# Relative attention on one core: content products moved to the free 64 rows, value products issued before the position products

## The chip, the cores and the metric

The program runs on one NeuronCore of one Trainium2 chip. The metric is the device time of one execution in microseconds (us); lower is better. The engines are PE (TensorE: matrix products, with its weight loads listed apart as PEld), DVE (VectorE), ACT (ScalarE), POOL (GpSimd) and SP (SyncE, which only issues transfers). SBUF is the on-chip working memory, PSUM the eight banks that PE writes its products into. A PE weight array has 128 rows, over which a product sums, and 128 columns, one per output row; a product may use only a part of either.

## The reference

The reference is a small network over x of shape (8, 512, 128): an attention block, a causal attention with a mixture of experts, a relative attention, and a low-rank feed-forward block, each with a layer norm. The change touches only the relative attention. Cut to what matters, for each of 8 sequences and 16 heads of width 8:

```python
AC = jnp.einsum('bhid,bhjd->bhij', q + u_bias[None, :, None, :], k)      # content
BD = jnp.einsum('bhid,hjd->bhij', q + v_bias[None, :, None, :], rp)      # positions
BD = _rel_shift(BD)
attn = jax.nn.softmax((AC + BD) * scale, axis=-1)
out = jnp.einsum('bhij,bhjd->bhid', attn, v)
```

## The kernel before

The program is a row of phases, each with its own semaphores and buffers; a phase starts when the one before has ended on all engines. `phase_relative` (from L1737) is the phase of the change. It works in 32 steps (8 sequences by 4 groups of 4 heads). A step has 16 tiles u = 0 to 15: tile u is head u // 4 and block u % 4 of 128 queries, against all 512 keys. The first four steps and the last four are written out, the 24 between them are a loop of six passes of four steps (`steps`, L1799).

Queries and keys are split into bf16 terms stacked to 48 rows (SK), so a product over 48 rows gives the float32 product. Four kinds of PE work occur in each step n:

- content (`content_tile`, L1920): one product of 128 queries with 512 keys into PSUM bank ps_ac[u % 2]. The tiles qu and k have 128 rows: rows 0 to 47 hold the stacks, and the rest are zeros set once by DVE at the start of the phase (L2056 to L2058). The product sums over all 128 rows.
- turn (`turn_tile`, L1927): four 128x128 float32 transposes of the finished scores into ps_keys[u % 2].
- positions (`wide_bank`, L1911): bf16 products of 48 rows by 32 columns, 8 to 20 of them to a bank of 512, for step n + 2. The queries with the v bias (qv) lie in rows 0 to 47 for even steps and in rows 64 to 111 for odd ones; the positions r are stored in both places. ACT copies each bank out (`copy_wide`, L1988), sends it to DRAM in two halves a step (`send`, L1993), and SP fetches it back skewed by one element a row (`fetch`, L1831), which is the relative shift. It lands in `shifted`.
- value (`value_head`, L1938): 32 float32 products of 128 rows by 9 columns per head, at u = 5, 9, 13 and, for the last head, at u = 1 of the next step.

For each tile DVE adds content and shifted positions with the row maximum (L2043) and subtracts the maximum (L2051); ACT takes the exponential of the turned tile (L2009). PE waits with content tile u + 2 for DVE to be done with tile u (two ps_ac banks), with turn tile u for L2051 of u and for the exponential of u - 2, and with a value head for the exponentials of its head, the last of them that of tile u - 2. A positions bank waits for ACT to have copied the bank three before it.

The order on PE is written out by hand. For each u of a step, cut to its calls:

```python
content_tile(n, s, u + 2)          # or the first two tiles of step n + 1
turn_tile(n, s, u)
wide_bank(n + 2, (j + 2) % NG, s, u // HT, u % HT)   # twice at u = 7 and 15
if u == 1 and not first:
    value_head(n - 1, 1 - s, G - 1)
if u % NT == 1 and u > NT:
    value_head(n, s, u // NT - 1)
```

SP issues, in order: at the start qv for two steps, ident, r (L1866), then a wait for all three settings of DVE (pad_set) and the stacks of step 0 (`load`, L1817 and L1819); in each step the stacks of the next step once the last head of the step before is done, the results, and the two fetches, each behind waits for the sending and for the turns that free its buffer.

Of the kernel before, what the change touches and what calls it, by code (L numbers as in the profile page):

```python
# [5 lines left out]
F32 = mybir.dt.float32  # L6
# [7 lines left out]
P = 128  # L14
NB = 8
L = 512
NT = L // P
H = 16
DH = 8
G = 4  # L20
# [5 lines left out]
SK = DH * len(TERMS_Q)  # L26
# [110 lines left out]
def phase_attention(nc, sems, x_in, w_qkvT, w_fcT, b_fc, gamma, beta, ident_in, x1_out, z1_out):  # L137

    SCALE = P ** -0.5
    with ExitStack() as ctx:
# [472 lines left out]
def phase_causal(nc, sems, q_stacks, k_stacks, v9_in, mask_in, maskT_in, ident_in, ctx_out):  # L615

    SCALE = DH ** -0.5
    ROWS = 64  # L620
# [1116 lines left out]
def phase_relative(nc, sems, qu_stacks, qv_stacks, k_stacks, v9_in, r_stack, ident_in, skew_dram, ctx_out):  # L1737
# [2 lines left out]

    SCALE = DH ** -0.5
    BANK = 512
    NBK = -(-CW // BANK)
# [2 lines left out]
    ROWS = 64  # L1748
    LOWEST = -3.0e38
    assert NBK == HT + 1 and NBK % BANKS == 0 and STEP == NG  # L1750
    with ExitStack() as ctx:  # L1751
        def sb(name, shape, dt=F32):
            return ctx.enter_context(nc.sbuf_tensor("r_" + name, shape, dt))
# [8 lines left out]
        qu = sb("qu", [P, 2, G, L], BF16)  # L1762
        k = sb("k", [P, 2, G, L], BF16)
# [10 lines left out]
        ps_ac = [bank("ps_ac0"), bank("ps_ac1")]  # L1774
# [4 lines left out]
        pad_set = sem("pad_set")  # L1779
# [33 lines left out]
        @block.sync  # L1813
        def _(sp):
            def load(it, j):
                for dst, src in ((qu, qu_stacks), (k, k_stacks)):
                    sp.dma_start(dst[0:SK, j % 2, :, :],  # L1817
                                 src.rearrange("b r (g h) t -> b g r h t", h=G)[it, j]).then_inc(loaded[j % 2], 16)
                sp.dma_start(v9[:, j % 2, :, :], v9_in.rearrange("b p t (g v) -> b g p t v", g=NG)[it, j])\  # L1819
                    .then_inc(loaded[j % 2], 16)  # L1820

            def load_queries(it, j):
                at = ROWS * (j % 2)
                sp.dma_start(qv[at:at + SK, :, 0:L], qv_stacks.rearrange("b r (g h) t -> b g r h t", h=G)[it, j])\
                    .then_inc(qv_loaded[j % 2], 16)

            def fetch(it, j, c):

                sp.wait_ge(sent[j % 2][c], 16 * uses(it, j))
                src = skew_dram[j % 2][c]  # L1830
                sp.dma_start(shifted[:, j % 2, HT * c:HT * (c + 1), :],  # L1831
                             bass.AP(tensor=src.tensor, offset=src.offset + P - 1, ap=[[CW - 1, P], [W, HT], [1, L]]))\
                    .then_inc(skewed[j % 2][c], 16)

            def after(it, j, by):
                return it + (j + by) // STEP, (j + by) % STEP

            def step(it, j, first, left):
                n = STEP * it + j
                if left >= 1:  # L1840
                    sp.wait_ge(head_done, G * n + 2)
                    load(*after(it, j, 1))
                if not first:
                    store(n - 1)
                if left >= 1:
                    if not first:
                        sp.wait_ge(keys_ps, TG * n)
                    fetch(*after(it, j, 1), 1)
                if left >= 2:
                    sp.wait_ge(keys_ps, TG * n + HT)  # L1850
                    fetch(*after(it, j, 2), 0)
                if left >= 4:
                    sp.wait_ge(wide_ps, 2 * NBK * (n + 3))
                    load_queries(*after(it, j, 4))

            def store(n):
                sp.wait_ge(out_sb, n + 2)
                for b in range(NT):
                    sp.dma_start(ctx_out[n, :, :, b * P:(b + 1) * P].rearrange("h r i -> r h i"),
                                 osb[Q * b:Q * b + VW, :, :]).then_inc(stored, 16)  # L1860

            load_queries(0, 0)
            load_queries(0, 1)
            sp.dma_start(ident[:, :], ident_in).then_inc(consts, 16)
            for s in range(2):
                sp.dma_start(r[ROWS * s:ROWS * s + SK, :, :, :],  # L1866
                             r_stack.rearrange("r (o g h) t -> g r o h t", g=2, h=G)[s]).then_inc(r_loaded, 16)
            sp.wait_ge(pad_set, 3)
            load(0, 0)
            sp.sem_inc(stored, 64)  # L1870
            for c in range(2):
                fetch(0, 0, c)
            sp.wait_ge(wide_ps, 2 * NBK)
            load_queries(0, 2)
            fetch(0, 1, 0)
            sp.wait_ge(wide_ps, 4 * NBK)
            load_queries(0, 3)
            steps(step, sp)
            store(NI - 1)
            for s in range(2):  # L1880
                sp.wait_ge(loaded[s], 48 * (NI // 2))
                sp.wait_ge(qv_loaded[s], 16 * (NI // 2))
                for c in range(2):
                    sp.wait_ge(sent[s][c], 16 * (NI // 2))
                    sp.wait_ge(skewed[s][c], 16 * (NI // 2))
            sp.wait_ge(r_loaded, 32)
            sp.wait_ge(stored, 64 * (NI + 1))

        @block.tensor
        def _(pe):  # L1890
# [26 lines left out]
            def content_tile(n, s, u):  # L1917
                h, b = u // NT, u % NT
                pe.wait_ge(ac_used, TG * n + u + 1)
                pe.matmul(ps_ac[u % 2][:, :], qu[:, s, h, b * P:(b + 1) * P], k[:, s, h, :], start=True, stop=True)\  # L1920
                    .then_inc(ac_ps, 1)

            def turn_tile(n, s, u):
                pe.wait_ge(s_ready, TG * n + u + 1)
                pe.wait_ge(exp_done, TG * n + u + 1)
                for j in range(NT):
                    last = pe.transpose(ps_keys[u % 2][:, j * P:(j + 1) * P],  # L1927
                                        shifted[:, s, u, j * P:(j + 1) * P], ident[:, :])
                last.then_inc(keys_ps, 1)
# [13 lines left out]
            def step(it, j, first, left):  # L1943

                n, s = STEP * it + j, j % 2
                for u in range(TG):
                    if u + 2 < TG:
                        content_tile(n, s, u + 2)
                    elif left >= 1:
                        if u + 2 == TG:  # L1950
                            pe.wait_ge(loaded[1 - s], 48 * uses(it + (j + 1) // STEP, (j + 1) % STEP))
                        content_tile(n + 1, 1 - s, u + 2 - TG)
                    turn_tile(n, s, u)
                    if left >= 2:
                        if u == 0:
                            pe.wait_ge(qv_loaded[s], 16 * (uses(it, j) + 1))
                        wide_bank(n + 2, (j + 2) % NG, s, u // HT, u % HT)
                        if u % HT == HT - 1:
                            wide_bank(n + 2, (j + 2) % NG, s, u // HT, HT)
                    if u == 1 and not first:  # L1960
                        value_head(n - 1, 1 - s, G - 1)
                    if u % NT == 1 and u > NT:
                        value_head(n, s, u // NT - 1)

            pe.wait_ge(consts, 16)

            for ps in (ps_out, *ps_wide):
                for j in range(NT):
                    last = pe.transpose(ps[:, j * P:(j + 1) * P], ident[:, :], ident[:, :])
            pe.wait_ge(pad_set, 3)  # L1970
            pe.wait_ge(r_loaded, 32)
            for n in range(2):
                pe.wait_ge(qv_loaded[n], 16)
# [59 lines left out]
        @block.vector  # L2033
        def _(dve):
            def step(it, j, first, left):
                n, s = STEP * it + j, j % 2
                for u in range(TG):

                    if u % HT == 0:
                        dve.wait_ge(skewed[s][u // HT], 16 * uses(it, j))  # L2040
                    dve.wait_ge(ac_ps, TG * n + u + 1)
                    dve.sem_inc(marks, 1)
                    dve.tensor_tensor_reduce(out=shifted[:, s, u, :], in0=ps_ac[u % 2][:, :],  # L2043
                                             in1=shifted[:, s, u, :], scale=1.0, scalar=LOWEST,
                                             op0=ALU.add, op1=ALU.max, accum_out=mx[:, u:u + 1])\
                        .then_inc(ac_used, 1)
                    take_maximum(n, s, u)

            def take_maximum(n, s, u):
                dve.wait_ge(ac_used, TG * n + u + 3)  # L2050
                dve.tensor_scalar(shifted[:, s, u, :], shifted[:, s, u, :], mx[:, u:u + 1], None,  # L2051
                                  ALU.subtract).then_inc(s_ready, 1)


            dve.memset(qv[:, :, L:L + 2], 0.0).then_inc(pad_set, 1)
            for stack in (qu, k):  # L2056
                dve.memset(stack[:, :, :, :].rearrange("p s h t -> p (s h t)").bitcast(F32), 0.0)\
                    .then_inc(pad_set, 1)  # L2058
            dve.sem_inc(head_done, 2)
            dve.sem_inc(ac_used, 2)  # L2060
            steps(step, dve)
# [107 lines left out]
```

## Time and profile before

| what | value |
|---|---|
| median of 3 runs | 2327.81 us (2321.74 to 2329.93) |
| the profiled execution's own time | 2317.44 us |
| span of its profile | 2315.8 us |
| PE, DVE, ACT busy over the span | 70%, 61%, 47% |
| relative attention: first step to last | about 1285 us to 2175 us of the span |

The time of a run is that of the whole execution; the span is the part that the profile covers. Busy shares are means over phases with different limits, so the stretch of the relative attention is read by itself. PE's products overlap and their ends are modelled by the profiler, so where PE's speed matters, starts are compared with starts. PEclk is TensorE's granted clock as a share of 2.4 GHz; it is either 1.0 (2.4 GHz) or 0.5 (1.2 GHz), and a value between is a mean over a stretch. Some product records are missing: of 512 content products the trace has 325. Releasers are inferred from semaphore numbers, so a wait of DVE in this phase may carry the name of a transfer of an earlier phase (c_q<-c_mrow).

### The profile page before, as it was taken

How to read it: one execution, taken by the hardware profiler on the slowest of the kernel's cores; microseconds unless marked ns; L12 is line 12 of the kernel's file. 1: busy time of each engine (PE TensorE's matmuls, PEld its weight loads, DVE VectorE, ACT ScalarE, POOL GpSimd, SP SyncE). 2: the span in 40 equal slices, each digit the busy share in tenths (PEclk: the TensorE clock that was granted, in tenths of full speed). 3: DMA queues.
4: the chain of work that ended last, by engine and by line, in shares of the span. 5: the costliest groups of instructions: out<-in, count | busy, mean ns of one | idle time of the engine just before them, and what ended most of it. 6: DMA issues, size and time to landing. Idle time of an engine off the chain costs nothing. (4 is left out here: it accounts for less than half of the span.)

```text
span 2315.8 us, 56802 instructions
## 1 busy us (share of the span) xinstructions
PE 1621.8 (70%) x20395; PEld 1101.1 (48%) x20583; DVE 1417.5 (61%) x3148; ACT 1099.5 (47%) x2028; POOL 358.5 (15%) x346
## 2 busy tenths in 40 slices
PE   5434278888724887888553688878787888878537
PEld 2212146666523666666322365555555555555423
DVE  4763376666366877777431376666666666666646
ACT  3332235656602443344242476666666666666303
POOL 1322200000043444444321000000000000000013
PEclk8766668999956998888875699989898889899859
DMA  1115522222155121111188999989999989999441
GB/s 37 41 41 182 181 62 60 51 60 58 31 163 172 46 87 51 60 50 50 52 263 223 318 358 360 344 316 352 318 367 315 368 305 362 320 362 343 157 148 55
DMA packets 220945, 433.41 MB, mean 187 GB/s; under 512 B 54736, under 2 KB 116080, under 8 KB 211280
## 3 DMA queue, kind: packets, MB, share of 16 engines
q1 hardware_dynamic: 202928, 263.61, 37.4%
q10 hardware_dynamic: 12672, 152.05, 15.9%
q0 software_dynamic: 5088, 14.16, 2.1%
q8 instruction: 181, 2.97, 0.6%
q14 instruction: 76, 0.62, 0.1%
HBM read 225.93 MB, written 203.55 MB: 185 GB/s over the span
## 5 line engine op out<-in xcount | busy, mean ns | idle before, releaser
L2043 DVE CUSTOM_DVE_ANT_0 r_shifted<-r_ps_ac,r_shifted 128x512 f32<-128x512 f32 x512 | 352.2, 688 | 324.0 <-PE r_ps_ac L1920 168.1
L2009 ACT ACTIVATE r_probs<-r_ps_keys 128x512 f32<-128x512 f32 x512 | 309.1, 604 | 275.9 <-PE r_ps_keys L1927 228.1
L1927 PE MATMUL r_ps_keys<-r_ident,r_shifted 128*128 128x128 f32 x2048 | 337.5, 290 | 63.0 <-issue 18.7
L1988 ACT ACTIVATE r_wide<-r_ps_wide 128x512 f32<-128x512 f32 (+1 forms) x576 | 328.8, 590 | 77.6 <-PE r_ps_wide L1911 76.7
L1927 PEld LDWEIGHTS r_ps_keys<-r_ident,r_shifted 128*128 128x128 f32 x2048 | 275.1, 150 | 64.9 <-issue 16.5
L1911 PE MATMUL r_ps_wide<-r_r,r_qv 48*32 48x96 bf16 (+12 forms) x6144 | 238.5, 258 | 58.8 <-issue 44.5
L2051 DVE TENSOR_SCALAR r_shifted<-r_shifted,r_mx 128x512 f32<-128x512 f32 x512 | 249.2, 487 | 18.3
L873 DVE TENSOR_REDUCE c_mx<-c_ps_rows 128x2 f32<-128x256 f32 (+3 forms) x256 | 198.0, 817 | 101.7 <-PE c_ps_rows L744 101.0
L846 ACT ACTIVATE c_probs<-c_ps_keys 128x512 f32<-128x512 f32 (+1 forms) x384 | 180.5, 530 | 141.8 <-PE c_ps_keys L744 138.4
L1248 POOL TENSOR_TENSOR e_gu_half<-e_weighed,e_gu_half 128x1024 fp32r<-128x1024 f32 x64 | 155.6, 2433 | 198.6 <-ACT e_gu_half L1383 198.0
L1911 PEld LDWEIGHTS r_ps_wide<-r_r,r_qv 48*32 48x32 bf16 x6144 | 103.4, 95 | 165.3 <-issue 164.1
L1938 PE MATMUL r_ps_out<-r_probs,r_v 128*9 128x128 f32 x4096 | 152.7, 287 | 25.4 <-issue 22.8
L1377 ACT ACTIVATE e_silu<-e_ps_a 128x1024 f32<-128x1024 f32 x64 | 65.8, 1028 | 220.0 <-PE e_ps_a L1308 192.5
L773 PE MATMUL c_ps_keys<-c_q,c_k 50*128 50x512 bf16 (+3 forms) x512 | 127.6, 321 | 42.9 <-DMA c_q<-c_mrow 25.0
L1920 PE MATMUL r_ps_ac<-r_k,r_qu 128*128 128x512 bf16 x325 | 134.8, 415 | 28.1 <-issue 27.6
L124 POOL MEMSET n_norm_consts<- 128x4 f32 x1 | 0.1, 101 | 947.3 <-POOLq L1751 947.3
L1466 DVE TENSOR_TENSOR e_weighed<-e_gu,e_weight_all 128x1024 f32<-128x1024 f32 x64 | 142.3, 2223 | 7.2 <-POOL e_gu_half L1248 0.5
L754 PE MATMUL c_ps_rows<-c_k,c_q 48*128 48x128 bf16 (+3 forms) x512 | 103.1, 332 | 48.0 <-DMA c_v<-v 40.0
L1938 PEld LDWEIGHTS r_ps_out<-r_probs,r_v 128*9 128x9 f32 x4096 | 104.5, 94 | 56.0 <-issue 40.5
L1324 PE MATMUL e_ps_o<-e_gu_half,e_w_half 128*128 128x512 f32 x384 | 120.7, 457 | 8.7 <-POOL e_gu_half L1248 8.7
L1308 PE MATMUL e_ps_b<-e_hT_half,e_w_half 128*128 128x512 f32 x384 | 107.8, 418 | 17.3 <-DVE e_gu L1459 16.8
L1459 DVE TENSOR_TENSOR e_gu<-e_silu,e_ps_b 128x1024 f32<-128x1024 f32 x64 | 77.8, 1215 | 67.0 <-PE e_ps_b L1308 66.4
(200 smaller groups left out, 2452.9 us busy)
## 6 DMA issues: line engine op xcount, KB each, us to landing
skew<-r_wide ACTq DMA_DIRECT2D x64, 2224.0 KB, 11.8
r_shifted<-skew SPq DMA_DIRECT2D x64, 2048.0 KB, 17.2
e_weight_all<-weights SPq DMA_DIRECT2D x8, 2048.0 KB, 7.1
stack<-d_part SPq DMA_DIRECT2D x96, 128.0 KB, 2.7
stack<-b_part SPq DMA_DIRECT2D x48, 128.0 KB, 3.5
stack<-b_part POOLq DMA_DIRECT2D x48, 128.0 KB, 3.6
c_q<-stack SPq DMA_DIRECT2D x64, 96.0 KB, 2.2
c_k<-stack SPq DMA_DIRECT2D x64, 96.0 KB, 2.2
```

Of the source, the lines that this page charges most:

```text
L846: act.activation(probs[:, p, e, at:at + width], ps_keys[f % BANKS][:, 0:width], ACT.Exp, scale=SCALE)\
L873: dve.tensor_reduce(mx[:, s % 2, :].rearrange("i (e m) -> i m e", e=2)[:, NT * p + b, :], ps_rows[b % 2][:, :, 0:(b + 1) * P], AX_X, ALU.m ...
L1248: pool.tensor_tensor(gu_halves[1][:, e % 4, :, :], weighed[:, e % 2, :, :], gu_halves[0][:, e % 4, :, :], ALU.subtract).then_inc(gu_low, 1)
L1466: dve.tensor_tensor(weighed[:, e % 2, :, :], gu[:, e % 2, :, :], weight_all[:, s, e, :].unsqueeze(1).broadcast_to([P, KH, L]), ALU.mult)\
L1911: last = pe.matmul(ps[Q * a:Q * a + Q, frm - lo:to - lo], qv[rows, h, q0 + one:q0 + one + Q], r[rows, g // 2, h, at:at + to - frm], start= ...
L1920: pe.matmul(ps_ac[u % 2][:, :], qu[:, s, h, b * P:(b + 1) * P], k[:, s, h, :], start=True, stop=True)\
L1927: last = pe.transpose(ps_keys[u % 2][:, j * P:(j + 1) * P], shifted[:, s, u, j * P:(j + 1) * P], ident[:, :])
L1938: last = pe.matmul(ps_out[Q * b:Q * b + VW, h * P:(h + 1) * P], v9[:, s, j, h * VW:(h + 1) * VW], probs[:, h % 2, j, b * P:(b + 1) * P], s ...
L1988: act.activation(wide[:, s, c, lo:hi], ps_wide[bk % BANKS][:, 0:hi - lo], ACT.Copy).then_inc(wide_sb, 1)
L2009: act.activation(probs[:, h % 2, :, b * P:(b + 1) * P], ps_keys[u % 2][:, :].rearrange("p (j i) -> p j i", j=NT), ACT.Exp, scale=SCALE).th ...
L2043: dve.tensor_tensor_reduce(out=shifted[:, s, u, :], in0=ps_ac[u % 2][:, :], in1=shifted[:, s, u, :], scale=1.0, scalar=LOWEST, op0=ALU.add ...
L2051: dve.tensor_scalar(shifted[:, s, u, :], shifted[:, s, u, :], mx[:, u:u + 1], None, ALU.subtract).then_inc(s_ready, 1)
```

## The change

The stacks of queries and keys are loaded into rows 64 to 111 for even steps and rows 0 to 47 for odd ones, opposite to the rows that qv of the same parity lies in. The content product sums over those 48 rows alone. DVE no longer sets the two tiles to zero, and SP and PE no longer wait for it. On PE the value products of a tile stand behind its turn and ahead of its positions bank.

```diff
             def load(it, j):
+                at = ROWS * (1 - j % 2)
                 for dst, src in ((qu, qu_stacks), (k, k_stacks)):
-                    sp.dma_start(dst[0:SK, j % 2, :, :],
+                    sp.dma_start(dst[at:at + SK, j % 2, :, :],
...
-            sp.wait_ge(pad_set, 3)
             load(0, 0)
...
                 pe.wait_ge(ac_used, TG * n + u + 1)
-                pe.matmul(ps_ac[u % 2][:, :], qu[:, s, h, b * P:(b + 1) * P], k[:, s, h, :], start=True, stop=True)\
+                rows = slice(ROWS * (1 - s), ROWS * (1 - s) + SK)
+                pe.matmul(ps_ac[u % 2][:, :], qu[rows, s, h, b * P:(b + 1) * P], k[rows, s, h, :], start=True,
+                          stop=True)\
                     .then_inc(ac_ps, 1)
...
                     turn_tile(n, s, u)
+                    if u == 1 and not first:
+                        value_head(n - 1, 1 - s, G - 1)
+                    if u % NT == 1 and u > NT:
+                        value_head(n, s, u // NT - 1)
                     if left >= 2:
...
                             wide_bank(n + 2, (j + 2) % NG, s, u // HT, HT)
-                    if u == 1 and not first:
-                        value_head(n - 1, 1 - s, G - 1)
-                    if u % NT == 1 and u > NT:
-                        value_head(n, s, u // NT - 1)
...
-            pe.wait_ge(pad_set, 3)
+            pe.wait_ge(pad_set, 1)
...
             dve.memset(qv[:, :, L:L + 2], 0.0).then_inc(pad_set, 1)
-            for stack in (qu, k):
-                dve.memset(stack[:, :, :, :].rearrange("p s h t -> p (s h t)").bitcast(F32), 0.0)\
-                    .then_inc(pad_set, 1)
```

## Rows read from the trace of the kernel before

**Rows 1.** Stretches: us, busy by engine (instructions), granted clock, DMA share, GB/s.
```profile
1284.90:2175.00 890.10, 729.35 (x12217) 484.77 (x12406) 581.97 (x1536) 571.37 (x1085) 0.00 (x0) 0.89 0.96 334
1406.60:1512.90 106.30, 89.71 (x1579) 59.77 (x1602) 72.76 (x192) 72.99 (x140) 0.00 (x0) 0.96 1.03 357
1512.90:2081.20 568.30, 462.55 (x7882) 307.52 (x8000) 364.33 (x960) 367.16 (x700) 0.00 (x0) 0.89 0.97 338
1525.00:1530.00 5.00, 3.72 (x45) 2.09 (x44) 0.56 (x1) 0.60 (x1) 0.00 (x0) 0.50 0.58 199
```

**Rows 2.** Timeline of DVE: start, length, instruction, in brackets idle before it.
```profile
1554.46 0.68 DVE L2043 CUSTOM_DVE_ANT_0 r_shifted<-r_ps_ac,r_shifted 128x512 f32<-128x512 f32 x1
...
1555.59 0.68 DVE L2043 CUSTOM_DVE_ANT_0 r_shifted<-r_ps_ac,r_shifted 128x512 f32<-128x512 f32 x1
...
1557.56 0.69 DVE L2043 CUSTOM_DVE_ANT_0 r_shifted<-r_ps_ac,r_shifted 128x512 f32<-128x512 f32 x1 [0.75 <-DMA c_q<-c_mrow]
```

**Rows 3.** Timeline of PE at the full clock; a row of xN ends with its last.
```profile
1506.09 0.39 PE L1920 MATMUL r_ps_ac<-r_k,r_qu 128*128 128x512 bf16 x1
1506.32 0.60 PE L1927 MATMUL r_ps_keys<-r_ident,r_shifted 128*128 128x128 f32 x4
1506.85 0.42 PE L1911 MATMUL r_ps_wide<-r_r,r_qv 48*32 48x96 bf16 x16
1507.20 0.39 PE L1920 MATMUL r_ps_ac<-r_k,r_qu 128*128 128x512 bf16 x1
...
1556.00 1.06 PE L1938 MATMUL r_ps_out<-r_probs,r_v 128*9 128x128 f32 x32
1557.22 0.60 PE L1927 MATMUL r_ps_keys<-r_ident,r_shifted 128*128 128x128 f32 x4 [0.16 <-ACT r_wide L1988]
```

**Rows 4.** DMA queues, 1300 to 2130 us: packets, MB, share of 16 engines.
```profile
q1 hardware_dynamic: 92220, 145.53, 57.6%
q10 hardware_dynamic: 8421, 133.32, 38.7%
```

**Rows 5.** Line 1927: duration in ns min/median/max.
```profile
L1927 PE MATMUL r_ps_keys<-r_ident,r_shifted x2048: 269/273/476, 1286.3 to 2173.5; 128*128 128x128 f32 x187
```

**Rows 6.** Timeline of PE behind a long stall, at half the clock.
```profile
1520.62 0.60 PE L1920 MATMUL r_ps_ac<-r_k,r_qu 128*128 128x512 bf16 x1 [5.82 <-issue]
1521.02 1.06 PE L1927 MATMUL r_ps_keys<-r_ident,r_shifted 128*128 128x128 f32 x4
1522.01 0.63 PE L1911 MATMUL r_ps_wide<-r_r,r_qv 48*32 48x32 bf16 x8
1522.97 0.42 PE L1927 MATMUL r_ps_keys<-r_ident,r_shifted 128*128 128x128 f32 x1 [0.33 <-DVE r_shifted L2051]
```

**Rows 7.** Timeline of PE in the causal phase, at the full clock.
```profile
328.58 0.39 PE L754 MATMUL c_ps_rows<-c_k,c_q 48*128 48x512 bf16 x2
...
354.88 0.19 PE L744 MATMUL c_ps_rows<-c_halves 64*128 64x64 bf16 x1
...
355.20 0.26 PE L744 MATMUL c_ps_rows<-c_halves 64*128 64x128 bf16 x4
355.40 0.28 PE L763 MATMUL c_ps_out<-c_ident,c_mx 128*16 128x128 f32 x1
```

**Rows 8.** The page's group of ACT's copies of the positions.
```profile
L1988 ACT ACTIVATE r_wide<-r_ps_wide 128x512 f32<-128x512 f32 (+1 forms) x576 | 328.8, 590 | 77.6 <-PE r_ps_wide L1911 76.7
```

**Rows 9.** Timeline of all engines at the start of the phase.
```profile
1244.95 1.76 DVE L2057 MEMSET r_qu<- 128x2048 f32 x1 [0.39 <-issue]
1245.79 1.31 SPq L1866 DMA_DIRECT2D r_r<-r_stack  x2
...
1248.88 0.34 SPq L1817 DMA_DIRECT2D r_qu<-stack  x1
...
1259.53 0.83 PE L1911 MATMUL r_ps_wide<-r_r,r_qv 48*32 48x32 bf16 x15 [7.07 <-issue]
...
1284.99 0.69 DVE L2043 CUSTOM_DVE_ANT_0 r_shifted<-r_ps_ac,r_shifted 128x512 f32<-128x512 f32 x1 [36.14 <-DMA c_q<-c_mrow]
```

## The prediction

> **What bounds the kernel now.** I read first the stretch of the relative attention by itself, then DVE and PE tile by tile inside it, then the transfer queues, and last the start of the phase.
>
> The stretch of the 32 steps takes 890.1 us, 27.8 us a step, at a mean granted clock of 0.89 [rows 1]. No engine is busy all the time, but the 16 DMA engines are at 0.96 of their time [rows 1], and the two queues that carry the positions out and back account for 57.6% and 38.7% of it [rows 4].
>
> DVE needs 1.13 us a tile when nothing holds it (1554.46 to 1555.59), and 1.97 us for the tile behind a value head (1555.59 to 1557.56, 0.75 us of it idle) [rows 2]. Four tiles thus take 3 x 1.13 + 1.97 = 5.4 us and a step 21.4 us where nothing stalls. That pace is PE's: from one content product to the next takes 1.11 us without a value head (1506.09 to 1507.20), and a value head adds its 32 products, 1556.00 to about 1557.0, since the turn that follows a content product starts 0.23 us behind it [rows 3]. PE's four tiles are 4 x 1.11 + 1.0 = 5.4 us, the same sum. PE may run only two content tiles ahead of DVE, but it is never far enough ahead to wait long; so each 0.1 us that PE gains or loses on a tile is 0.1 us of the unstalled step.
>
> The other 6.4 us of a step are stalls. One kind is PE's, at the beginning of a loop pass: 5.82 us in which it waits for nothing that the profile shows, behind which the clock is 0.5 (1.2 GHz) [rows 6]. The rest is transfers that land late. So two limits lie close together: PE's tile, and transfers that are full nearly all the time. The pass of 106.3 us without the long stalls ran the DMA engines at 1.03, the five passes after it, which have them, took 568.3 / 5 = 113.7 us at 0.97 [rows 1].
>
> **The change, part by part.**
>
> *Content product over 48 rows.* The product streams 512 columns whatever its rows. In the causal phase a 48-row product of 512 columns takes the same 0.39 us as the 128-row one here [rows 3, 7]. Cost of its own: 0.
>
> *The switch from content to turn.* Before, both use the whole array (128*128), and the turn starts 0.23 us after the content product, which is little over the 0.213 us that 512 columns take at 2.4 GHz [rows 3]. Where the shape changes, the trace shows more. Four turns start at 1506.32 and end their row 0.60 us later; one lasts 0.27 [rows 5], so they start (0.60 - 0.27) / 3 = 0.11 us apart and the last at 1506.65; the positions products, 48*32, start at 1506.85, 0.20 us later, 0.09 more than the pace [rows 3]. From positions to content it is the same: the last of 16 starts at about 1507.00, streams 256 columns or 0.11 us, and content starts at 1507.20 [rows 3]. The nearest row to the new switch is in the causal phase, from 64*128 products to a transpose over 128 rows: the last of four starts about 355.28 (0.26 less the 0.19 that one of 64 columns lasts), has 64 columns or 0.03 us, and the transpose starts at 355.40, again 0.09 us late [rows 7]. At half the clock: four turns 0.21 us apart ((1.06 - 0.42) / 3), the last at 1521.66, positions at 1522.01, so 0.14 us [rows 6]. All 512 content products are followed by a turn. A mean clock of 0.89 is 22% of the time at 0.5 [rows 1], so the new switch costs 512 x (0.78 x 0.09 + 0.22 x 0.14) = 52 us of PE time. Bounds: 0, if 64 and 128 rows are no different shape, and 52.
>
> *The switch from positions to content.* It stays a change of columns, 32 to 128, but the two now lie in opposite row halves. What that is worth no row shows. Two products of one shape in opposite halves start together, the two of 512 columns within 0.01 us (the pair's row is 0.39 long, as one alone) [rows 7]. If the same held across shapes, content would start as the last positions product does, 0.20 us earlier, in the 30 steps that have positions: 480 x 0.20 = 96 us less. If a change of shape waits for everything in the array, it is 0. I take 0: in each change of shape that the trace shows, the wait is the same 0.09 us whatever the two shapes are, which looks like emptying the array and not like a conflict of rows. That is the step I am least sure of.
>
> The Trainium skill, TensorEngine Tiling (Array Packing), section Key Properties, says that changing the tiling mode, and not merely the tile, drains the engine; by it the 52 us come and the 96 us do not. The 0.09 us of rows 3 and 7 agree with it for shapes that share rows; none here has disjoint ones.
>
> *Value heads ahead of the positions.* The same number of shape changes in a tile (turn, value, positions, content against turn, positions, value, content). The value head needs the exponential of tile u - 2, which the turn before it already waited for: no new wait. Queued behind it now is one positions bank, and ACT's copy of it (0.59 us [rows 8]) comes about 1 us later. Until then ACT is idle, since its next exponential is for a turn that stands behind the value head in both orders. Cost 0, with ACT's slack as the cover; if that cover were gone, 0.59 us a head, 128 heads, 76 us, of which I see nothing. No bank sent to DRAM (u = 7 and 15) is in a value tile. The heads end up to 0.4 us sooner, so SP may load the next stacks that much sooner, 30 times: 0 to -2 us.
>
> *The start.* Two settings of 1.76 us go from DVE, which then waits until 1284.99 in any case: 0 [rows 9]. SP's wait for them ends just ahead of 1248.88; now the three loads of step 0 can follow the r transfers, issued until 1247.10, so 1.8 us earlier. PE starts at 1259.53, when r has landed, not when the zeros are set [rows 9]. The loads come behind r in the queue: 0, between -1.8 and +1.8 us if the bytes that move ahead of it gain or lose what they take. SP, PE and POOL have no other change; bytes and packets are the same, since only the rows they land in differ.
>
> *What of the 52 us reaches the end.* The transfers are the cover. The passes give the exchange rate. A pass with a long stall loses some 10 us at it (5.82 in the row shown [rows 6], and over 4 more from 1525, where DVE works 0.56 us of 5 and the DMA share falls to 0.58 [rows 1]) and, through the clock (0.89 for 0.96), about 4 us more; it takes 113.7 - 106.3 = 7.4 us longer. So half of an addition to PE's time is hidden by transfers. Those additions come in one lump, behind which the DMA engines run dry for some us; the new ones are spread over all tiles and leave them full, so somewhat more should be hidden. I take 0.4: 52 x 0.4 = 21 us. Bounds 0 and 52.
>
> **Sum.** 21 for the switch, 0 for all else: the profiled execution would go from 2317.4 to 2338 us. It is 10.4 us under the median of the runs shown, 2327.8, so against the median I predict 2327.8 + 21 = 2349 us. A measurement of this kernel can tell about 0.3%, 7 us, from no change.
>
> **The rivals.**
>
> 1. *Opposite halves work side by side across shapes* (the other side). Place: between a positions bank and the content product behind it. Price: 96 us less, 52 more for the switch to the turn, net -44 us of PE time, of which half shows: -22 us, 2306 us. It decides if the 0.20 us between the last positions product and content falls below 0.10. For it: rows 7's pair. Against: every change of shape seen waited. The Trainium skill, TensorE: Matmul & The Clock Gate, Part 3, ties the overlap of weight loads with running products to differing row groups and says nothing of equal shapes; by that this rival holds. Chance 0.25.
> 2. *Transfers hide it all.* With the DMA engines at 0.96 to 1.03 [rows 1] either sign may vanish: 2328 us. Against: half of the long stalls does show. Chance 0.22.
> 3. *The change doesn't do what it says*: 48 rows are run as if they were 128, with no new switch and no overlap. The intervals stay, and so does the time, 2328 us. Rows 7's transpose speaks against it. Chance 0.08.
>
> My forecast has 0.45.
>
> **How the numbers follow.** Slower by over 0.3%: 0.38 of the forecast's 0.45 (the rest hidden further), and 0.06 of the others: 0.44. Faster: 0.22 of rival 1 and 0.04 of the others: 0.26. Within 0.3%: 0.30. The range goes from rival 1 with a little over half of it showing, 2302 us, to nearly all 52 us unhidden, 2376 us; with both signs in it, the forecast's own range is 2328 to 2376 us.
>
> **What would show it.** Right: turn starts 0.32 us behind content where it was 0.23; positions to content stays 0.20; the tile at full clock is 1.20 us on PE for 1.11; DVE's idle time for ps_ac grows; the DMA share falls a little under 0.96. Rival 1: content starts within 0.1 us of the last positions product, and the DMA share goes to 1. Rival 2: the tile on PE longer or shorter, and the stretch still 890 us. Wrong altogether: long stalls that move or multiply, or a lower granted clock at the same tile pace.

## The result, and the profile after

The changed kernel takes 2449.15 us, median of four executions (2423.73 to 2493.8), against 2328.87 us for the kernel before; the ratio is 1.0437 with a 95% interval of 1.0366 to 1.0508. Slower was forecast, but by 21 us: the loss is 120 us, and the time lies above the range of 2302 to 2376 us. The four executions differ far more than those of before, and in step with the granted clock: 2424 us at a mean clock of 0.787, 2437 at 0.775, 2461 at 0.768, 2494 at 0.758. (The ratio leaves out the longest ones, and by it the loss is 102 us; medians here are over all executions, since their clock is part of what is looked for.)

The changed kernel's stretch of the relative attention and two pieces of it; the columns are those of [rows 1]:

```profile
1282.40:2280.90 998.50, 915.94 (x12383) 511.07 (x12382) 604.48 (x1536) 590.55 (x1084) 0.00 (x0) 0.80 0.85 298
1432.60:1460.90 28.30, 24.87 (x401) 14.36 (x400) 18.98 (x48) 18.62 (x35) 0.00 (x0) 0.99 1.03 374
1660.00:1736.00 76.00, 75.65 (x740) 39.16 (x740) 33.19 (x84) 34.91 (x61) 0.00 (x0) 0.50 0.62 219
```

The stretch is 108 us longer than in [rows 1], which is the whole difference of the two spans (2422.1 and 2315.8). Its clock is 0.80 for 0.89. As the clock is 1.0 or 0.5, a share of 2 x (1 - clock) of a stretch is at half of it: 40% of 998.5 us, 399 us, where before it was 22% of 890.1, 196 us. The second row is one step at the full clock: 28.3 us with the DMA engines at 1.03, as good as an average step before. The third is 76 us without a break at half the clock: PE is busy throughout, DVE less than half the time, and the DMA share is down to 0.62. There PE alone sets the pace: DVE's 84 instructions are those of 28 tiles, so a step of 16 takes 43 us.

The page's groups that answer to the main lines, DVE's of the kernel before first, then those of the changed kernel:

```profile
L2043 DVE CUSTOM_DVE_ANT_0 r_shifted<-r_ps_ac,r_shifted 128x512 f32<-128x512 f32 x512 | 352.2, 688 | 324.0 <-PE r_ps_ac L1920 168.1
...
L2046 DVE CUSTOM_DVE_ANT_0 r_shifted<-r_ps_ac,r_shifted 128x512 f32<-128x512 f32 x512 | 354.0, 691 | 416.3 <-PE r_ps_ac L1922 410.8
L1991 ACT ACTIVATE r_wide<-r_ps_wide 128x512 f32<-128x512 f32 (+1 forms) x576 | 325.4, 583 | 192.5 <-PE r_ps_wide L1912 191.6
L1922 PE MATMUL r_ps_ac<-r_k,r_qu 48*128 48x512 bf16 x512 | 226.8, 443 | 38.7 <-issue 27.7
```

DVE is now idle for 416 us ahead of its additions, 411 of it for content products, where it was 324 and 168 before, and ACT's copies of the positions 192 us where [rows 8] had 77. Each copy still takes 0.58 us, so nothing on the other engines has become dearer; they wait for PE.

PE's timeline in the changed kernel, first at the full clock, then at half:

```profile
1566.48 0.39 PE L1922 MATMUL r_ps_ac<-r_k,r_qu 48*128 48x512 bf16 x1
1566.80 0.66 PE L1930 MATMUL r_ps_keys<-r_ident,r_shifted 128*128 128x128 f32 x4
1567.39 0.40 PE L1912 MATMUL r_ps_wide<-r_r,r_qv 48*32 48x288 bf16 x8
1567.72 0.39 PE L1922 MATMUL r_ps_ac<-r_k,r_qu 48*128 48x512 bf16 x1
...
1706.80 0.60 PE L1922 MATMUL r_ps_ac<-r_k,r_qu 48*128 48x512 bf16 x1
1707.34 1.11 PE L1930 MATMUL r_ps_keys<-r_ident,r_shifted 128*128 128x128 f32 x4
1708.38 0.62 PE L1912 MATMUL r_ps_wide<-r_r,r_qv 48*32 48x192 bf16 x8
1708.93 0.60 PE L1922 MATMUL r_ps_ac<-r_k,r_qu 48*128 48x512 bf16 x1
```

The turn starts 0.32 us behind content for 0.23 [rows 3], and its row of four is 0.66 us long for 0.60. From content to content it is 1.24 us; a tile of the same 8 positions products took 1.09 us before. At half the clock the turn starts 0.54 us behind content for 0.40 [rows 6], and the tile takes 2.13 us. The weight loads of the four turns tell where the longer row comes from, before (content at 1506.09 [rows 3]) and changed (content at 1566.48):

```profile
1506.10 0.57 PEld L1927 LDWEIGHTS r_ps_keys<-r_ident,r_shifted 128*128 128x128 f32 x4
...
1566.80 0.42 PEld L1930 LDWEIGHTS r_ps_keys<-r_ident,r_shifted 128*128 128x128 f32 x4 [0.23 <-issue]
```

Before, the first load starts 0.01 us behind content; now it starts 0.32 us behind it, with the turn itself.

From the last positions product to content nothing has changed: eight products end their row 0.40 us after 1567.39, the last starts 0.13 us in, and content starts 0.20 us behind it although it lies in the other row half.

### The profile page after: what moved, and what is told of

It is laid out like the page before. It is cut to its first block and busy times, and to the rows that moved or that the text cites. A ratio compares the mean times of both kernels' runs of the same rounds, so it can differ in the third digit from the quotient of the medians.

```text
span 2422.1 us, 56987 instructions
## 1 busy us (share of the span) xinstructions
PE 1803.4 (74%) x20582; PEld 1127.1 (47%) x20583; DVE 1435.7 (59%) x3146; ACT 1118.4 (46%) x2028; POOL 358.7 (15%) x346
## 5 line engine op out<-in xcount | busy, mean ns | idle before, releaser
L1930 PE MATMUL r_ps_keys<-r_ident,r_shifted 128*128 128x128 f32 x2048 | 396.5, 324 | 12.2 <-issue 11.0
L1930 PEld LDWEIGHTS r_ps_keys<-r_ident,r_shifted 128*128 128x128 f32 x2048 | 252.6, 160 | 147.4 <-issue 142.2
L1912 PE MATMUL r_ps_wide<-r_r,r_qv 48*32 48x96 bf16 (+12 forms) x6144 | 251.9, 272 | 34.4 <-issue 20.2
L1922 PE MATMUL r_ps_ac<-r_k,r_qu 48*128 48x512 bf16 x512 | 226.8, 443 | 38.7 <-issue 27.7
L1912 PEld LDWEIGHTS r_ps_wide<-r_r,r_qv 48*32 48x32 bf16 x6144 | 108.8, 99 | 163.0 <-issue 161.6
L1941 PE MATMUL r_ps_out<-r_probs,r_v 128*9 128x128 f32 x4096 | 171.6, 313 | 12.8 <-issue 12.0
L1941 PEld LDWEIGHTS r_ps_out<-r_probs,r_v 128*9 128x9 f32 x4096 | 111.3, 101 | 56.7 <-issue 40.6
```

What stands on the lines that cost most here:

```text
L1912: last = pe.matmul(ps[Q * a:Q * a + Q, frm - lo:to - lo], qv[rows, h, q0 + one:q0 + one + Q], r[rows, g // 2, h, at:at + to - frm], start= ...
L1922: pe.matmul(ps_ac[u % 2][:, :], qu[rows, s, h, b * P:(b + 1) * P], k[rows, s, h, :], start=True, stop=True)\
L1930: last = pe.transpose(ps_keys[u % 2][:, j * P:(j + 1) * P], shifted[:, s, u, j * P:(j + 1) * P], ident[:, :])
L1941: last = pe.matmul(ps_out[Q * b:Q * b + VW, h * P:(h + 1) * P], v9[:, s, j, h * VW:(h + 1) * VW], probs[:, h % 2, j, b * P:(b + 1) * P], s ...
```

## The experiments

Three theories went in. S: the switch of shape from content to turn costs PE time, and the clock is lost with it. R: a content product in fewer rows brings less clock. O: the value heads' new place is at fault. Fifteen kernels ran. In the table, the stretch is that of the profiled execution from the first addition of DVE to the last, the time at half the clock is twice its missing clock times its length, and the tile is PE's time from one content product to the next (in e4, where content and positions mix, from one turn to the next) at the full clock with 8 positions products and no value head between (median).

| kernel | median us (runs) | ratio, interval | stretch us | clock | at half us | DMA share | tile us |
|---|---|---|---|---|---|---|---|
| before | 2329 to 2333 | 1 | 890 | 0.89 | 196 | 0.96 | 1.09 |
| changed | 2449 (4) | 1.044, 1.037 to 1.051 | 998 | 0.80 | 399 | 0.85 | 1.24 |
| e1 rows only | 2385 (4) | 1.016, 1.008 to 1.024 | 991 | 0.79 | 416 | 0.86 | 1.24 |
| e2 order only | 2336 (10) | 1.002, 1.000 to 1.004 | 907 | 0.89 | 200 | 0.94 | 1.09 |
| e3 one more switch | 2329 (10) | 1.001, 0.998 to 1.004 | 891 | 0.92 | 143 | 0.96 | 1.20 |
| e4 content in quarters | 2411 (4) | 1.034, 1.028 to 1.039 | 973 | 0.82 | 350 | 0.88 | 0.94 |
| e5 66 rows | 2342 (10) | 1.005, 1.003 to 1.008 | 910 | 0.86 | 255 | 0.94 | 1.09 |
| e6 64 rows | 2374 (4) | 1.013, 1.006 to 1.020 | 965 | 0.83 | 328 | 0.89 | 1.24 |
| e7 twice, 128 rows | 2331 (10) | 0.999, 0.996 to 1.001 | 895 | 0.95 | 90 | 0.96 | 1.30 |
| e8 twice, 48 rows | 2395 (4) | 1.027, 1.024 to 1.031 | 948 | 0.94 | 114 | 0.91 | 1.45 |
| e9 48 rows, one half | 2391 (4) | 1.026, 1.021 to 1.030 | 956 | 0.84 | 306 | 0.90 | 1.24 |
| e10 changed again | 2459 (5) | 1.051, 1.046 to 1.056 | 1066 | 0.72 | 597 | 0.79 | 1.24 |
| e11 rows only again | 2394 (4) | 1.011, 1.002 to 1.020 | 993 | 0.80 | 397 | 0.85 | 1.24 |
| e12 three quarters fetched | 2280 (4) | 0.976, 0.972 to 0.980 | 857 | 0.91 | 154 | 0.91 | 1.09 |
| e13 the same, twice 128 rows | 2302 (4) | 0.987, 0.985 to 0.989 | 877 | 0.96 | 70 | 0.89 | 1.30 |
| e14 one in four threefold | 2375 (4) | 1.016, 1.011 to 1.021 | 948 | 0.90 | 190 | 0.90 | 1.24 |
| e15 another in four | 2366 (4) | 1.017, 1.014 to 1.019 | 926 | 0.91 | 167 | 0.93 | 1.24 |

The profiled executions of e1, e6, e10, e11 and e14 are among the longer ones of their kernel, those of the changed kernel, e8 and e15 the shortest or nearly so, so their rows stand above or below what the medians beside them would have.

A mean over the stretch mixes the two levels of the clock. Counting DVE's tiles by the clock under which they pass, from the same traces (stalls fall to the level in which they lie; the time at half comes out within 10 us of the table's):

| kernel | steps of 32 at half the clock | us a step at full | us a step at half |
|---|---|---|---|
| before | 3.7 | 24.7 | 51 |
| changed | 8.4 | 25.6 | 47 |
| e3 | 3.1 | 25.7 | 47 |
| e5 | 5.1 | 24.2 | 50 |
| e6 | 6.6 | 25.3 | 49 |
| e7 | 1.3 | 26.3 | 68 |
| e8 | 1.9 | 27.7 | 59 |
| e9 | 6.5 | 25.2 | 48 |
| e10 | 13.1 | 25.1 | 45 |

At the full clock the changed kernel's step is only 0.9 us longer. What it loses comes from 4.7 more steps at half the clock, each about 21 us longer than at full: some 100 of the 108 us.

**Which part of the change (e1, e2).** e1 is the changed kernel with the value heads back behind the positions bank; e2 is the kernel before with this alone:

```diff
                     turn_tile(n, s, u)
+                    if u == 1 and not first:
+                        value_head(n - 1, 1 - s, G - 1)
+                    if u % NT == 1 and u > NT:
+                        value_head(n, s, u // NT - 1)
                     if left >= 2:
```

> The content products over 48 rows in the opposite half, with the order of before (value heads behind the positions bank). Theory S (the switch of shape from content to turn costs PE 0.146 us at full clock, 0.09 for emptying the array and 0.056 for a weight load that can no longer be made ahead, and the clock is lost with it): all of the loss is here, 2435 to 2490 us, content tile to content tile 1.24 us where no value head lies between. Theory O (the value heads ahead of the positions are to blame): back near 2330 us.

> The kernel before with the value heads ahead of the positions bank and nothing else. Theory S: no new switch, 2322 to 2336 us, tile to tile 1.09 us. Theory O: 2400 us or more.

The order alone costs at most 0.4%. The rows, with the switch that they bring, cost 54 us by the median (26 to 38 by the ratios of e11 and e1; 2341 to 2426 us over their eight executions), which is not "all of the loss": the two together cost 120. S as written fails on that; O fails for the kernel with 128 rows.

**A switch without fewer rows (e3).** One product more, ahead of content, 32 columns of the array wide and overwritten by it:

```diff
+                pe.matmul(ps_ac[u % 2][0:Q, 0:1], qu[:, s, h, 0:Q], k[:, s, h, 0:1], start=True, stop=True,
+                          skip_group_check=True)
                 pe.matmul(ps_ac[u % 2][:, :], qu[:, s, h, b * P:(b + 1) * P], k[:, s, h, :], start=True, stop=True)\
```

> The kernel before, content over all 128 rows, with one product of 128 rows by 32 columns and one column of data ahead of each content product, overwritten by it: a second switch of shape in each tile that has no value head ahead of it. It tells what lowers the clock. Theory S (switches, in which the array stands still): about 0.1 us more a tile and long stretches at 0.5 as in the changed kernel, 2400 us or more. Theory R (48 rows for 128 count as less work of the array): 0.1 us more a tile, some 2345 us, and the share of the stretch at half the clock stays near the 21% of before.

e3's timeline of PE, and its stretch:

```profile
1600.45 0.18 PE L1920 MATMUL r_ps_ac<-r_k,r_qu 128*32 128x1 bf16 x1
1600.56 0.39 PE L1922 MATMUL r_ps_ac<-r_k,r_qu 128*128 128x512 bf16 x1
1600.78 0.60 PE L1929 MATMUL r_ps_keys<-r_ident,r_shifted 128*128 128x128 f32 x4
1601.31 0.40 PE L1911 MATMUL r_ps_wide<-r_r,r_qv 48*32 48x192 bf16 x8
1601.64 0.18 PE L1920 MATMUL r_ps_ac<-r_k,r_qu 128*32 128x1 bf16 x1
```

```profile
1290.90:2182.00 891.10, 752.20 (x12652) 525.84 (x12900) 600.52 (x1536) 572.30 (x1084) 0.00 (x0) 0.92 0.96 334
```

The extra switch is there, content 0.11 us behind a product of a single column, and the tile is 0.105 us longer in the 12 of 16 tiles that have no value head ahead of content: 384 x 0.105 = 40 us of PE time. The time does not move (interval 0.998 to 1.004), nor does the stretch, and the clock is no lower. So this switch brings no loss of clock. It does not show that 40 us are hidden whole: a step at the full clock is 1.0 us longer, and time at half the clock is 53 us shorter, which makes up for it. The added product also works over 128 rows, and the late weight load of the changed kernel is not in e3, so a switch with no product beside it was not tried.

**Do opposite halves work side by side (e4).** Content as four products of the positions' own shape:

```diff
-                pe.matmul(ps_ac[u % 2][:, :], qu[rows, s, h, b * P:(b + 1) * P], k[rows, s, h, :], start=True,
-                          stop=True)\
-                    .then_inc(ac_ps, 1)
+                pe.sem_inc(bank_marks, 1)
+                for a in range(P // Q):
+                    last = pe.matmul(ps_ac[u % 2][Q * a:Q * a + Q, :],
+                                     qu[rows, s, h, b * P + a * Q:b * P + a * Q + Q], k[rows, s, h, :],
+                                     start=True, stop=True, skip_group_check=True)
+                last.then_inc(ac_ps, 1)
```

> The changed kernel with the content product split into four of 48 rows by 32 columns, the shape of the positions products, so that positions and content differ only in their row half. Theory S with overlap inside one shape: content starts with the last positions products, 0.2 us earlier, against 0.146 us at the turn: tile to tile 1.03 to 1.06 us, near or under before, 2300 to 2340 us if the clock comes back. Rival (opposite halves give nothing even in one shape): the tile stays at 1.15 us or more and the time over 2400 us. Theory R: the tile is short, but the clock stays at 0.5 for as long as in the changed kernel, about 2400 us.

e4's timeline (rows of PE, PEld and DVE), at full clock and at a stall behind the next head:

```profile
1610.59 0.69 DVE L2049 CUSTOM_DVE_ANT_0 r_shifted<-r_ps_ac,r_shifted 128x512 f32<-128x512 f32 x1
...
1610.89 0.25 PE L1912 MATMUL r_ps_wide<-r_r,r_qv 48*32 48x32 bf16 x4
...
1610.92 0.40 PE L1924 MATMUL r_ps_ac<-r_k,r_qu 48*32 48x512 bf16 x4
...
1610.93 0.37 PE L1912 MATMUL r_ps_wide<-r_r,r_qv 48*32 48x384 bf16 x4
...
1611.24 0.66 PE L1933 MATMUL r_ps_keys<-r_ident,r_shifted 128*128 128x128 f32 x4
...
1611.72 0.68 DVE L2049 CUSTOM_DVE_ANT_0 r_shifted<-r_ps_ac,r_shifted 128x512 f32<-128x512 f32 x1
...
1616.62 0.13 PEld L1924 LDWEIGHTS r_ps_ac<-r_k,r_qu 48*32 48x32 bf16 x4 [2.67 <-issue]
```

Inside one shape they do: content starts 0.03 us behind the first positions products, between them, and the next turn 0.35 us behind those. The tile is 0.94 us, shorter than S had it. This is what the prediction's first rival wanted, and it needs equal shapes, not only opposite halves. It still loses 3.4%, as R had forecast: the clock is 0.82, with 350 us at half. Stalls such as the last row, in which PE waits for nothing that the profile shows, stand in the tiles behind the value heads: behind three of the four heads of a step DVE's interval is 3.0 to 3.2 us for 2.0 to 2.1 before (medians). What feeds these stalls was not tried; e4 also issues 1536 more products. Where no head lies between, DVE's interval stays 1.13 us (1610.59 to 1611.72), as in [rows 2]: that is what DVE itself needs for a tile, so a PE tile under 1.13 us brings nothing there.

**How many rows (e5, e6, e9).** Content of the kernel before over 66, 64 or 48 rows from row 0, the zeros left in place:

```diff
-                pe.matmul(ps_ac[u % 2][:, :], qu[:, s, h, b * P:(b + 1) * P], k[:, s, h, :], start=True, stop=True)\
+                pe.matmul(ps_ac[u % 2][:, :], qu[0:66, s, h, b * P:(b + 1) * P], k[0:66, s, h, :], start=True, stop=True)\
```

> The kernel before, content summed over rows 0 to 65 for 0 to 127 (18 of them zeros): the shape of the array that the product takes stays that of 128 rows, so there is no new switch, but few more rows work than in the changed kernel. Theory R, by rows (what the clock is granted for is the rows that a product works in): 350 us or more of the stretch at half the clock and 2360 us or more, at 1.09 us a tile. Theory R, by shape (it is the half of the array that the product is placed in): as before, 150 to 200 us at half the clock, 2320 to 2340 us.

> The same with rows 0 to 63: two rows less than e5, and now the shape of 64 rows, with the switch to the turn. Both theories R: 350 us or more of the stretch at half the clock, 1.24 us a tile at full clock, 2360 to 2460 us. If only 48 rows against 64 mattered it would be near 2330 us.

> The kernel before, content over rows 0 to 47 for every step: the switch and the 48 rows of the changed kernel, but neither the alternating half nor the new order. Theory R (fewer working rows, lower granted clock): mean clock under the 0.797 to 0.819 of 64 rows, 2370 to 2450 us. Rival H (content in the half opposite to the positions is what hurts): like 64 rows, 2347 to 2389 us.

The stretches of e5 (first) and e6:

```profile
1286.70:2197.00 910.30, 788.67 (x12415) 497.51 (x12414) 583.32 (x1536) 572.94 (x1085) 0.00 (x0) 0.86 0.94 327
```

```profile
1281.40:2246.00 964.60, 882.97 (x12411) 497.90 (x12414) 604.48 (x1536) 578.45 (x1085) 0.00 (x0) 0.83 0.89 308
```

66 rows keep the shape, the tile of 1.09 us and all 512 columns; only rows that held zeros are gone. The mean clock of the whole execution is 0.800 to 0.808 in the ten executions (mean 0.803), against 0.808 to 0.823 (mean 0.816) for the kernel before beside it on the same chip, and the time is 0.5% up; 1 lies outside the interval (1.003 to 1.008). Neither form of R had it right: it lies between the two. With 64 rows and the switch, the clock of the execution is 0.797 to 0.819, no lower than with 66, but the time is 1.3% up. As the two differ by two rows of zeros and the switch from content to turn, on one chip, it is the switch that costs here (2347 to 2389 us for 2332 to 2351). That it does so while the clock is low, when PE needs 2.13 us a tile for 1.94, fits but is not shown apart. With 48 rows the clock is 0.799 to 0.800 and the time 2391 us, like e1 and e11, whose halves alternate (rival H falls). R's time came, its sign did not: the clock lies within that of 64 rows, not under it. So of the 2.6% that 48 rows cost, the rows alone are shown for the 0.5% of e5; 48 rows without the switch were not tried (e9's tile of 1.24 us has it, like that of 64 rows).

**More work on purpose (e7, e8).** Each content product issued twice, over 128 rows in the kernel before and over 48 in the changed one:

```diff
+                pe.matmul(ps_ac[u % 2][:, :], qu[:, s, h, b * P:(b + 1) * P], k[:, s, h, :], start=True, stop=True)
                 pe.matmul(ps_ac[u % 2][:, :], qu[:, s, h, b * P:(b + 1) * P], k[:, s, h, :], start=True, stop=True)\
```

> The kernel before with each content product issued twice over 128 rows, the second overwriting the first: 0.21 us more of PE's time in each of the 512 tiles, 109 us in all, with the array at work in it. e3 added 0.105 us to 3 tiles of 4 and no time. If transfers cover PE's pace at full clock up to this: 2330 to 2350 us. If e3 was at the edge of the cover: 2380 to 2430 us. Time at half the clock under theory R: no longer than the 188 us of before.

> The changed kernel with each content product issued twice over its 48 rows. Theory R: the added columns in 48 rows do not bring the clock back as the 128 rows of e7 do; with 0.21 us more a tile (0.43 at half the clock), 2500 us or more. Rival (it is the share of the time in which the array streams anything that counts): the added streaming keeps the clock up, the stretch has 200 us or less at half the clock, and the time is under 2400 us.

The stretches of e7 and e8:

```profile
1292.80:2188.00 895.20, 823.79 (x12902) 512.10 (x12904) 605.09 (x1536) 572.16 (x1084) 0.00 (x0) 0.95 0.96 332
```

```profile
1293.30:2241.00 947.70, 909.48 (x12894) 471.86 (x12892) 604.99 (x1536) 587.62 (x1084) 0.00 (x0) 0.94 0.91 313
```

e7 puts 512 x 0.21 = 109 us of useless streaming on PE, and the time stays. Two effects cancel in it: a step at the full clock is 1.6 us longer, about half of the 3.4 that PE has more to do, and 106 us less pass at half the clock. e8 does the same to the changed kernel and is 54 to 64 us *faster* than it (2395 for 2449 and 2459): the clock is back, 114 us at half for 399 to 597. R had forecast that 48 rows would not bring it back; the rival in e8 was right about the clock (under 200 us at half) and barely about the time (2395, under 2400; 2385 to 2407). It is still 2.7% over the kernel before, because a tile of 1.45 us is more than transfers hide: most of its steps take 27.6 us, with PE busy for 0.96 of the stretch.

**Again, side by side (e10, e11).** The changed kernel and e1 once more on one chip.

> The changed kernel once more, beside the next one on one chip. If the value heads' place matters in it: its median at least 30 us over that of the order of before, as the first four runs of each had it (2449 and 2385). If that was chance: medians within 30 us of each other.

> The same rows with the order of before, once more: 2385 us if its first four runs were typical, up to 2450 us if the difference was chance.

e10's stretch:

```profile
1298.40:2364.00 1065.60, 1000.41 (x12415) 547.48 (x12414) 604.47 (x1536) 596.90 (x1085) 0.00 (x0) 0.72 0.79 279
```

2459 us (2444 to 2533) against 2394 (2341 to 2426): with 48 rows the order does cost some 65 us, and 597 of 1066 us pass at half the clock in the execution shown. Tiles are equally long in both orders (1.24 us, 2.24 with a value head), and at an equal mean clock the orders take equal time (2424 us at 0.787, 2437 at 0.775; in the order of before 2425 at 0.780), so the order acts through the clock.

**Are transfers the cover (e12, e13).** The kernel before, and e7, with three quarters of each row fetched; the last quarter is set to zero once:

```diff
-                sp.dma_start(shifted[:, j % 2, HT * c:HT * (c + 1), :],
-                             bass.AP(tensor=src.tensor, offset=src.offset + P - 1, ap=[[CW - 1, P], [W, HT], [1, L]]))\
+                sp.dma_start(shifted[:, j % 2, HT * c:HT * (c + 1), 0:3 * P],
+                             bass.AP(tensor=src.tensor, offset=src.offset + P - 1, ap=[[CW - 1, P], [W, HT], [1, 3 * P]]))\
```

> The kernel before with 384 of 512 columns of each row fetched back (the positions of the last 128 keys are left out), which takes a quarter off the fetches' bytes, some 12% of all in the stretch. If transfers bound the kernel before, and not PE's pace: 40 to 100 us less, 2230 to 2290 us. If PE's pace does: under 15 us less.

> The kernel with each 128-row content product issued twice (e7) and 384 of 512 columns fetched (e12; the positions of the last 128 keys are left out). If transfers are what hid 0.21 us a tile in e7, then with a quarter less to fetch that work must show: more than e12's 2280 us, up to 2330. If it still takes e12's time within 10 us, transfers bound both, and PE has yet more room.

e12 takes 2280 us (2269 to 2286), ratio 0.976, so transfers do bound much of the kernel before: with some 12% of the bytes gone from the stretch, 54 us go. e13 takes 2302 us (2296 to 2311): of the 109 us that e7 added at no loss, 23 show once the fetches are lighter, with 84 us less at half the clock beside them.

**Streaming beside or away from the value heads (e14, e15).** The changed kernel, with one content product of four issued three times:

```diff
+                for _ in range(2 if u % NT == 0 else 0):       # e15: == 2
+                    pe.matmul(ps_ac[u % 2][:, :], qu[rows, s, h, b * P:(b + 1) * P], k[rows, s, h, :], start=True,
+                              stop=True)
```

> The changed kernel with the content product of one tile in four issued three times over its 48 rows, the one directly behind a value head and its positions bank: 0.43 us more at full clock, four times a step. In the traces the clock comes back from 0.5 almost only beside value heads. If what PE does beside a head decides the return, the added streaming there shortens the stretches at half the clock well under the 390 to 590 us of the changed kernel: 2350 to 2400 us, and less than the next kernel by 20 us or more.

> The same three-fold product, for the content tile two tiles later, away from the heads. The same work. If the place decides: 20 us or more over the kernel before it in this list, 2400 to 2480 us. If only the amount of streaming does: both the same.

e15's stretch:

```profile
1286.10:2212.00 925.90, 871.25 (x12659) 484.81 (x12662) 604.56 (x1536) 589.64 (x1085) 0.00 (x0) 0.91 0.93 321
```

e14 takes 2375 us (2354 to 2383), e15 2366 (2354 to 2376): the place of the added products doesn't matter, against what was expected of e14, and in both some 80 us of the loss come back for 256 useless products. The test is a narrow one, for no tile is more than two from a head. In both, as in the changed kernel, every return from half to full (11, 11 and 12) lies within 3 us behind a value product, where about half of the time lies. That leaves the effect of the order with 48 rows shown but not explained.

## Why the prediction was wrong

Its direction and its first mechanism held. The step that failed is the clock: it was held at the 0.89 of before, and the cost was priced with one share for both of its levels.

- *The granted clock* was carried over, in "0.78 x 0.09 + 0.22 x 0.14" and in the length of the stretch. It fell to 0.80, and 8.4 of the 32 steps ran at half of it for 3.7. At 47 us a step for 25.6 those 4.7 steps are some 100 of the 108 us. The same goes for the others: against the kernel before, time at half the clock rose by 203 us in the changed kernel and the stretch by 108; in e10 by 401 and 176; in e9 by 110 and 66; in e6 by 132 and 75; in e5 by 59 and 20. That is 0.3 to 0.6 us of stretch for each, a quotient and not a price of the clock alone, since all but e5 have the longer tile too. "Wrong altogether: a lower granted clock" was named among the signs, without a chance of its own. Why the clock stays at half through 76 us in which PE is busy for 75.65 no run shows.
- *"What of the 52 us reaches the end", 0.4,* was read from passes that differed by a stall and by clock, so it mixed the two levels. At the full clock it is not far off: in the kernels with the 1.24 us tile a step is 0.2 to 0.9 us longer for 2.3 us of PE work. In the 76 us at half it is all of it: PE has no gap, and the DMA share is 0.62.
- *The switch from content to turn* was placed rightly and mis-sized. The turn starts 0.32 us behind content, as stated. But the four turns take 0.055 us longer as well, since the first turn's weights are no longer loaded under the content product. The cost is 0.146 us a tile for the 0.09 forecast, and 0.19 for 0.14 at half the clock; the same sum then gives 80 us of PE time instead of 52.
- *"That pace is PE's"* holds for the four tiles with their head, but not for a tile without one: DVE needs 1.13 us for it by itself, PE 1.09 to 1.11. So what PE gains on such a tile gains nothing, and of the 0.146 us that it lost DVE's interval shows 0.10 (1.24 for 1.14, medians).
- *The switch from positions to content* was the step called least sure: 0 taken, 0 found, in opposite halves too (0.20 us unchanged), and e4 shows that the wait goes when the shapes are the same. The Trainium skill, TensorEngine Tiling (Array Packing), Key Properties, has a change of mode drain the engine; the trace agrees.
- *Value heads ahead: cost 0* held in the kernel with 128 rows (e2) and failed in the changed one (e10, e11), by some 65 us.
- *Content over 48 rows costs 0 of its own* is right for its length, 0.39 us either way, and wrong for the kernel: 66 rows for 128 alone cost 0.5%. The Trainium skill, TensorE: Matmul & The Clock Gate, section Why this matters for your kernels, says that a product over 32 rows takes the time of one over 128; the trace agrees on the time, and e5 shows a price beside it.
- *The start*: r is issued and the stacks follow at once. From the first issue for qv to DVE's first addition it is 41.7 us for 40.6, so nothing is gained, and the difference is within the spread of the runs.
- Rival 2 (transfers hide it) fits the time of e3 and e7, but not e8, which kept its clock and lost 2.7%.

## What to carry to other kernels

Before PE work is taken away, look at whether PE's clock holds: where transfers set the pace, the streaming and the rows that look wasted (here zeros in 80 of 128 rows) may be what keeps the clock at its full level. Taking 62 of them out slowed this kernel by 0.5% without any instruction being longer; in the changed kernel the switch and the order came on top. Price a change of pace for the two levels of the clock apart, since what is hidden at one level may be bare at the other. Here products in different rows overlapped only where their shapes were the same as well, and each change of shape cost 0.09 us (0.14 at half the clock), and at the turn also the weight load that could no longer be made ahead.

## What the runs showed of the hardware

- Rows of zeros count for the clock. The same product in 66 rows instead of 128 lowered the execution's mean clock from about 0.816 to 0.803 and raised the time at half the clock in the stretch from 196 to 255 us.
- Streaming that computes nothing brings the clock back: 512 repeated products over 48 rows took the changed kernel from 399 to 114 us at half the clock, and 256 of them (e15) to about 167 us.
- One more change of shape, with a product of one column over 128 rows, in 384 tiles did not lower the clock: it was 0.92 in the stretch for 0.89.
- Weights of the next product were loaded under a running one of the same shape (0.01 us behind its start), and not across a change of shape (0.32 us).
- How long the clock stays low differs between executions of one kernel: the changed kernel ranged over 2424 to 2533 us in nine executions, e7, whose clock held, over 2316 to 2336 in ten.
